# Layer 0's first norms interleaved with the first quad's projections, and x loaded in eight parts

## The reference

```python
def _layernorm(x, axis=-1, eps=1e-5):
    m = jnp.mean(x, axis=axis, keepdims=True)
    v = jnp.var(x, axis=axis, keepdims=True)
    return (x - m) / jnp.sqrt(v + eps)
...
q = (hidden_states @ Wq).reshape(b, l, N_HEADS, FEAT_DIM).transpose(0, 2, 1, 3)
k = (hidden_states @ Wk).reshape(b, l, N_HEADS, FEAT_DIM).transpose(0, 2, 1, 3)
v = (hidden_states @ Wv).reshape(b, l, N_HEADS, V_DIM).transpose(0, 2, 1, 3)
qf = taylor_exp(q)
kf = taylor_exp(k)
A = jnp.einsum('bhnf,bhmf->bhnm', qf, kf)
A = jnp.tril(A)
y = jnp.einsum('bhnm,bhme->bhne', A, v)
...
x = x + _L0_attn_ref(_layernorm(x, axis=-1), L0_attn_Wq, L0_attn_Wk, L0_attn_Wv, L0_attn_Wo)
x = x + _L0_ffn_ref(_layernorm(x, axis=-1), L0_ffn_w_gate, L0_ffn_w_up, L0_ffn_w_down)
```

## Time and profile before

| | us |
|---|---|
| median of 3 runs | 2360.39 |
| the profiled execution | 2361.38 |
| its span (core 4, the slowest; first to last instruction) | 2359.9 |
| other cores' spans | 2347.9 to 2357.7 |
| quad 0's pieces start, core 4 | 36.10, 55.15, 75.39, 95.34 |
| first scores of attention, core 4 | 107.31 |

### The profile page before, as it was taken

One profiled execution on the slowest core, in us unless ns is written; L12 is line 12 of the kernel. 1 busy time (PEld: TensorE's weight loads), 2 busy tenths in 40 slices (PEclk: granted clock), 3 DMA queues, 4 the chain that ended last, 5 costly groups with the idle time before them and its releaser, 6 DMA issues. The chain is left out here.

```text
span 2359.9 us, 34886 instructions; the slowest of 8 cores (2347.9 to 2359.9 us)
## 1 busy us (share of the span) xinstructions
PE 1980.6 (84%) x12314; PEld 921.0 (39%) x12314; DVE 1165.7 (49%) x2056; ACT 1095.4 (46%) x1986; POOL 28.8 (1%) x72
## 2 busy tenths in 40 slices
PE   3688887888879999599998888877795499979999
PEld 2433333332334444244444444443442244434444
DVE  3222444433444542241463666666655688876442
ACT  3465555565431110011222777776743778874221
POOL 0000000000000000000000000000000000000000
PEclk9799878877889999799999899888797599989999
DMA  8001333440018850664001000000202122223332
GB/s 213 2 1 37 108 125 126 143 99 1 1 42 218 231 169 1 134 178 70 3 1 25 13 11 11 10 11 2 37 2 73 72 63 79 74 85 112 107 107 89
DMA packets 60071, 170.09 MB, mean 72 GB/s; under 512 B 3840, under 2 KB 36608, under 8 KB 48896
## 3 DMA queue, kind: packets, MB, share of 16 engines
q1 hardware_dynamic: 53536, 134.31, 16.9%
q0 software_dynamic: 6368, 33.56, 8.7%
HBM read 167.85 MB, written 33.55 MB: 85 GB/s over the span
## 5 line engine op out<-in xcount | busy, mean ns | idle before, releaser
L653 PE MATMUL f0R<-lnT,wgu 128*128 128x512 bf16 x1536 | 337.4, 383 | 27.9 <-DMA wgu<-f0wgu_d 27.9
L419 ACT ACTIVATE a0bq<-a0S 128x1024 bf16<-128x1024 f32 (+1 forms) x320 | 266.5, 894 | 191.2 <-PE a0S L344 190.6
L653 PEld LDWEIGHTS f0R<-lnT,wgu 128*128 128x128 bf16 x1536 | 151.7, 99 | 213.3 <-issue 35.7
L688 ACT ACTIVATE f0si<-f0R 128x1024 bf16<-128x1024 f32 x48 | 49.1, 1023 | 389.2 <-PE f0R L653 389.2
L1287 PE MATMUL g1hp<-g1q1T,g1t 128*128 128x512 bf16 x1024 | 225.0, 381 | 5.5 <-DVE g1a L1407 4.2
L1311 PE MATMUL g1hp<-g1t,g1q1T 128*128 128x512 fp8e4 x1024 | 222.9, 381 | 1.8 <-ACT g1q1T L1362 1.8
L361 PE MATMUL a0y<-a0bq,a0vv 128*64 128x512 bf16 (+3 forms) x640 | 131.5, 406 | 50.9 <-ACT a0bq L419 20.2
L714 DVE TENSOR_TENSOR f0hT<-f0si,f0R 128x1024 bf16<-128x1024 bf16 x48 | 58.6, 1222 | 227.9 <-PE f0R L653 227.9
L1084 ACT ACTIVATE a1pt<-a1T 128x768 bf16<-128x768 bf16 (+2 forms) x152 | 118.5, 785 | 113.0 <-PE a1T L969 102.8
L1287 PEld LDWEIGHTS g1hp<-g1q1T,g1t 128*128 128x128 fp8e4 x1024 | 98.4, 98 | 131.9 <-issue 19.2
L1311 PEld LDWEIGHTS g1hp<-g1t,g1q1T 128*128 128x128 bf16 x1024 | 100.5, 98 | 123.9 <-issue 4.2
(11 more groups left out here) (189 smaller groups left out, 2934.6 us busy)
## 6 DMA issues: line engine op xcount, KB each, us to landing
a0wst<-g1w_d SPq DMA_DIRECT2D x32, 1024.0 KB, 4.8
f0wst<-g1w_d SPq DMA_DIRECT2D x32, 1024.0 KB, 6.0
hs_scr<-g1hsp SPq DMA_DIRECT2D x32, 512.0 KB, 3.2
g1q1T<-hs_scr SPq DMA_DIRECT2D x8, 2048.0 KB, 10.5
wgu<-f0wgu_d POOLq DMA_DIRECT2D x24, 512.0 KB, 6.9
xs<-x SPq DMA_DIRECT2D x4, 2048.0 KB, 26.0
t_scr<-f0wt SPq DMA_DIRECT2D x32, 256.0 KB, 2.5
g1t<-t_scr SPq DMA_DIRECT2D x2, 4096.0 KB, 15.1
```

What stands on the lines that cost most here:

```text
L419: s.activation(bq[:, u % 4, :, n0:512], sS[:, u % 2, :, n0:512], AF.Square).then_inc(s_sq, 1)
L653: mm = t.matmul(R[:, k % 4, 512 * n2:512 * (n2 + 1)], wgu[:, cc % 3, x, j, :], lnT[:, j, t0 + 512 * n2:t0 + 512 * (n2 + 1)], start=(j == 0 ...
```

## The change

A new item L (the norm of one tile) enters the list. Four L items open it. Then, among quad 0's pieces, tile 4n+4 is put behind piece 4n+1, tile 4n+5 behind piece 4n+2, and tiles 4n+6 and 4n+7 behind piece 4n+3, for n = 0 to 2. The start of the list is L0 L1 L2 L3 P0 P1 L4 P2 L5 P3 L6 L7 P4 P5 L8 and so on. The rstd and `nb` are made for two tiles at a time, and VectorE takes the statistics of tile i+2 at item L of tile i.

x comes in eight parts of 1 MB. GpSimd sets the constants first, waits for part 1 of x, and then issues quad 0's weights. SyncE issues parts 0 and 1, waits for these weights, and issues parts 2 to 7 and then `qb`. Each piece 0, 4, 8 and 12 still waits for its four tiles, and VectorE still waits for `cstd` at piece 0.

```diff
-    out = [("P", 0, i) for i in range(A0_PIECES)]
+    out = [("L", ti) for ti in range(4)]
+    for i in range(A0_PIECES):
+        out.append(("P", 0, i))
+        if i < 12 and i % 4 > 0:
+            out += [("L", ti) for ti in range(i + 3, i + 4 + i % 4 // 3)]
...
-        l_x = [sem(f"x{g}") for g in range(4)]
+        l_x = [sem(f"x{g}") for g in range(8)]
...
             @blk.gpsimd
             def _(g):
-                g.dma_start(w0[:, 0, :, :], w0_d[0, :, :, :]).then_inc(wq[0], 16)
                 g.memset(eps[:, :], 2e-12)
...
                 g.drain().then_inc(cst, 1)
-                g.wait_ge(l_x[3], 16)
+                g.wait_ge(l_x[1], 16)
+                g.dma_start(w0[:, 0, :, :], w0_d[0, :, :, :]).then_inc(wq[0], 16)
+                g.wait_ge(l_x[7], 16)
                 for q in range(1, 4):
                     g.dma_start(w0[:, q, :, :], w0_d[q, :, :, :]).then_inc(wq[q], 16)
...
             @blk.sync
             def _(sp):
-                for g in range(4):
-                    sp.dma_start(xs[:, 4 * g:4 * g + 4, :],
-                                 x_in[512 * g:512 * (g + 1), :].rearrange("(n pp) m -> pp n m", pp=128)
+                for g in range(8):
+                    if g == 2:
+                        sp.wait_ge(wq[0], 16)
+                    sp.dma_start(xs[:, 2 * g:2 * g + 2, :],
+                                 x_in[256 * g:256 * (g + 1), :].rearrange("(n pp) m -> pp n m", pp=128)
                                  ).then_inc(l_x[g], 16)
                 sp.dma_start(qb[:, :], qb_d).then_inc(cstd, 16)
...
             @blk.tensor
...
-                    if it[0] == "P":
+                    if it[0] == "L":
+                        ti = it[1]
+                        if ti >= 2:
+                            t.wait_ge(N1.ev, ti - 1)
+                        norm_pe_transpose(t, N1, lsc, ident, as_tiles(sS[:, ti % 2, 0, :]), ti)
+                    elif it[0] == "P":
...
                         if g == 0 and i in (0, 4, 8, 12):
-                            for ti in range(i, i + 4):
-                                if ti >= 2:
-                                    t.wait_ge(N1.ev, ti - 1)
-                                norm_pe_transpose(t, N1, lsc, ident, as_tiles(sS[:, ti % 2, 0, :]), ti)
                             t.wait_ge(N1.ev, i + 4)
...
             @blk.scalar
...
+                    if it[0] == "L":
+                        ti = it[1]
+                        if ti % 2 == 0:
+                            norm_act_rstd(s, N1, ti, ti, 2)
+                            s.wait_ge(s_nb, ti // 2 + 1)
+                        if ti >= 2:
+                            s.wait_ge(N1.tp, ti - 1)
+                        s.activation(lsc[:, ti % 2, :], xs[:, ti, :], AF.Identity,
+                                     scale=N1.rstd[:, ti:ti + 1], bias=nb[:, ti:ti + 1]).then_inc(N1.ap, 1)
+                        if ti % 4 > 0:
+                            norm_act_evac(s, N1, lnT, as_tiles(sS[:, (ti - 1) % 2, 0, :]), ti - 1, ti - 1)
+                        if ti % 4 == 3:
+                            norm_act_evac(s, N1, lnT, as_tiles(sS[:, ti % 2, 0, :]), ti, ti)
...
             @blk.vector
...
-                for ti in range(4):
+                for ti in range(2):
                     norm_dve_stats(v, N1, xs, ti, ti)
                 for it in order:
-                    if it[0] == "P":
+                    if it[0] == "L":
+                        i = it[1]
+                        if i % 2 == 0:
+                            v.wait_ge(N1.rs, i + 2)
+                            v.scalar_tensor_tensor(nb[:, i:i + 2],
+                                                   N1.mv[:, i:i + 2, 0:1].rearrange("p a b -> p (a b)"),
+                                                   -1.0, N1.rstd[:, i:i + 2],
+                                                   ALU.mult, ALU.mult).then_inc(s_nb, 1)
+                        if i < 14:
+                            v.wait_ge(l_x[i // 2 + 1], 16)
+                            norm_dve_stats(v, N1, xs, i + 2, i + 2)
+                    elif it[0] == "P":
                         _, g, i = it
                         n = bank[it]
-                        if g == 0 and i in (0, 4, 8, 12):
-                            v.wait_ge(N1.rs, i + 4)
-                            v.scalar_tensor_tensor(nb[:, i:i + 4],
-                                                   N1.mv[:, i:i + 4, 0:1].rearrange("p a b -> p (a b)"),
-                                                   -1.0, N1.rstd[:, i:i + 4],
-                                                   ALU.mult, ALU.mult).then_inc(s_nb, 1)
-                            if i < 12:
-                                v.wait_ge(l_x[i // 4 + 1], 16)
-                                for ti in range(i + 4, i + 8):
-                                    norm_dve_stats(v, N1, xs, ti, ti)
-                            else:
-                                v.wait_ge(cstd, 16)
                         if g == 0 and i == 0:
                             v.wait_ge(cstd, 16)
                         v.wait_ge(s_pj, n + 1)
```

## The result

The changed kernel is slower: 2376.9 us, the median of its four runs, against 2361.3, now the median of four runs of the kernel before; ratio 1.0057, 95% interval 1.0035 to 1.0079, which is 13.5 us. Medians hold all runs of a kernel, here also a disturbed one of 2614.4 us (the other three have the median 2375.4), and ratios only the undisturbed ones; in the profile of e4_split one die was disturbed, so its numbers are those of cores 0 to 3.

The account below looks back on a forecast made before the run. Bound: the slowest core's own chain of waits. The wait for qb and two handovers a group start piece 12 8.5 us later, the rest unchanged, so 2360.4 becomes 2368.9 us; range 2358 to 2376, chance 0.80.

Parts of the forecast that it names:

- Opening: Before the first projections: short drain, first apply at 13.4, weights landed at 22.8, first pieces at about 23.5 instead of 36.1.
- The wait for qb: First evacuation: VectorE waits for qb, issued behind parts 2 to 7 of x, until 43.3, bare for more than 12 us.
- rival that qb does not bind: At the first evacuation: qb is served early, tile 4's transposes start at 34.5, total 2356.9 us; chance 0.09.
- early weights: Rival on quad 0's loading: weights land at 17.0, qb 5.8 us sooner, total 2363.1 us; chance 0.06.
- estimate of 4.4 us: Quad 0's 1 MB weight load by the skill's fit, 2.0 us plus bytes at 436 GB/s; the forecast used 10.6.
- third rival: At GpSimd's drain: its 14 us do not come from the weights, qb lands at 48.6, total 2374.2 us; chance 0.05.
- Group of tiles 4 to 7: After qb lands: tile 4's transposes at 46.45, piece 4 at 60.65 against 55.15 before.
- Two handovers a group: Groups 8 to 11 and 12 to 15: interleaving hides two norms but pays two handovers; 21.6 us a group taken.
- Front: Up to the start of piece 12: 103.85 instead of 95.34, 8.5 us later.
- All of the 2265 us behind follow unchanged.: Everything behind the front: later loads wait for TensorE's or VectorE's counts, so the rest only shifts.
- the 1.00 of the first stretch: Granted clock read for core 4's first two pieces of a group, though their matmuls run at the slow pace.

Follow-up runs that it names:

- e4_split: e1_qb_first with VectorE's and ScalarE's part of each norm one piece earlier in the list, TensorE's transposes left in place; ratio 0.9940 against the kernel before.
- e1_qb_first: The changed kernel with one line moved, so that SyncE issues qb ahead of part 0 of x; ratio 1.0008 against the kernel before.

## Why the prediction was right

The forecast was slower by 8.5 us; measured are 13.5. By the ratio that is 2373.8 us on the 2360.4 of before, inside the range; the bare median, 2376.9, lies 0.9 above its upper end of 2376. The steps:

- **Opening.** Drain gone, statistics at 8.2 (8.75 on core 3), apply 13.4 (14.06), projections 23.5 (24.14), weights landed 22.8 (21.9): all within 1 us.
- **The wait for qb.** Forecast at 43.3; the first evacuation came between 41.15 and 45.93 on the eight cores. e1_qb_first took the wait away and 11.6 us with it. The rival that qb does not bind is out, and so is that of early weights: they took 7.9 to 10.3 us from issue to landing on the eight cores, 9.7 on core 3. The estimate of 4.4 us from the fit in the Trainium skill (DMA: Bandwidth & Descriptors, Anatomy of one DMA) is not borne out by this trace, in which seven other cores load as well. The drain was short, so the third rival is out too.
- **Group of tiles 4 to 7.** 46.45 for the transposes and 60.65 for piece 4; core 3 had 48.23 and 62.13, 1.8 and 1.5 us late because qb landed 1.8 us late, with 13.9 us between them (14.2 forecast).
- **Two handovers a group.** Confirmed by rows (two gaps of 2.4 us) and by e4_split, which removes them. The later groups took 20.1 and 20.7 us on the mean, not 21.6. The waits are as forecast (2.46 and 6.9, for 2.4 and 6.8), and the clock fell in the middle in 8 of 16 groups, about as often as I took it for. Two terms were too large: pieces 2 and 3 with their transposes take 4.55 us where the clock holds and 6.0 to 6.2 where it fell (5.2 and up to 7.4 forecast), and the first two pieces 5.7 (6.15 forecast). The range has these groups' room the wrong way round: it is 2.3 up and 2.1 down.
- **Front.** Those two make +7.1 us in place of +8.5.
- **"All of the 2265 us behind follow unchanged."** This is the term that was mis-sized, put at nothing because all later loads wait for TensorE's or VectorE's counts, with no term for the clock: attention took 5.8 us more. Its instructions are the same, but TensorE's clock falls in gaps across which it held before (183.4 us at the low level, 166.0 before). In the stretch that was looked at, the loss goes with where the gap falls against the changes of the clock, and 39 of 40 cores with the interleaved list have it, against 7 of 32 with the block list. Why that list sets the gap there is not settled.

So the mechanism of the front was right. The total is 5 us short: the front was 1.4 us over, and what I had held to be a plain shift took 5.8 us more in attention. In the earlier trace rows, the 1.00 of the first stretch is no reading of the clock: core 4's trace has no clock record before 40.1 us, and the matmuls' own pace, as I took it, is what counts there.

## What to carry to other kernels

A wait has the price of its place in the queue: before delaying a bulk load, look at what small transfers are issued behind it on the same queue, and issue those first (here 0.5 KB behind 6 MB, 11.6 us). When work is interleaved in one list that several engines follow in order, each engine needs its own lead: the vector and scalar parts one piece ahead of the TensorE part, with qb first, turned an interleaving that gained nothing into a gain of 14 to 23 us. And a front that starts sooner is not yet time: read the granted clock of the stretches behind it.

## What the runs showed of the hardware that was not expected

- GpSimd's drain behind a transfer that it had issued itself lasted until that transfer had landed (17.23 against 17.06); without one in front, GpSimd was past it at 1.89. On the eight cores it ended 0.15 us behind the landing.
- The same 1.70 us gap with the same work around it left TensorE's clock at the full level (14.0 us, 1.00 granted) on some cores and kernels and at the low one (16.4 us, 0.81) on others. Hundredths of a microsecond separate the two: 14.0 with the last rise of the clock 5.28 to 5.49 us before the restart, 16.4 with 5.21 to 5.26. Over some 560 us such stretches add up to 5 or 6 us.
- A 0.5 KB transfer landed 2.1 us after issue at the head of the queue, and 18.7 us after issue behind six parts of x.
